# A plan drawn up with other weights: a transformer block with two attentions and a routed feed-forward, ordered by a list planner

## The chip, the cores and the metric

The kernel runs on one core of a Trainium2 chip. The core has a matrix engine (TensorE, PE in the profile, its weight loads PEld), a vector engine (VectorE, DVE), a scalar engine (ScalarE, ACT), GpSimd (POOL) and DMA queues (SyncE, SP, issues most of them). Each engine works through its own list of instructions in order, and semaphores tie the lists together. The metric is the device time of one execution in microseconds; the median of three runs of the kernel before is 718.24 us.

## The reference

Hidden states are 2048 tokens of 128 numbers. With LN a layer norm without weights, the kernel computes:

```
h  = LN(x)
h  = h + global_attention(rmsnorm(h) * w1)      # causal, 16 heads of 8, 4 key heads, latent keys and values
h  = h + local_attention(rmsnorm(h) * w2)       # the same heads, window of 32 tokens
x  = x + LN(h)
f  = LN(x) * gamma + beta
p  = softmax(f @ router.T); e = argmax(p)       # 8 experts
y  = silu(f @ T(sw1)) @ T(sw2) + max(p) * (silu(f @ T(ew1[e])) @ T(ew2[e]))
out = x + LN(y)
```

T() makes weights ternary: round(W / scale) in -1, 0, 1, times the scale of the row. In both attentions queries and keys get a rotary embedding and a norm per head.

## The kernel before

The tokens are worked on in 8 blocks (b = 0 to 7) of 256. For each block there is a front part for each attention (statistics, norm, transposes, projection, a Newton iteration on GpSimd for the head norms, a split into three bf16 parts, an expansion on GpSimd, transposes of keys and queries), the attention itself, an output part, the norms, and the feed-forward. The attention is cut into units (a, b, g, kb): attention a (0 global, 1 local), block b, key head group g of 4, key tile kb. A unit is a score product on TensorE ("qk"), the exponential on ScalarE, for tiles on the diagonal a mask on GpSimd, and later a product with the values ("pv"). Block b has 4 x (2b + 2) global units and 8 local ones, so the work per block grows.

Output steps are "oevac" (ScalarE copies the sums), "oT" (transposes, VectorE divides), "onT" (transposes, ScalarE copies) and "wo" (the output product and residual). Then come "fstat", "fxa", "fh" (the norms) and the 25 steps of ffn_steps: transposes "fhT", router "frouter", "fparts" (bf16 parts on VectorE), "fohT", "fmask" (the one-hot masks are transposed and multiplied into the inputs of the eight experts), first layer "fw1s" and "fw1" with "fz", "fact", "fh1", second layer "fw2" and "fw2s" with "fsel", and "fsum", "fout".

Nothing of the order is written by hand. make_plan() draws up one list of steps, PLAN, when the kernel is built, and each engine then issues its share of every step in that order. The planner keeps books: for each engine the time at which it is free, for three of the PSUM banks and the two score buffers the time at which they come free, and for each step the estimates of COST (engine and us, in order), with HOP = 0.537 us between engines. At every turn it takes the first step of each chain that is allowed (bank count, buffers read), computes the stall that it would cause, 0.98 per us of idle TensorE and 0.432 per us of any other engine, takes off the PULL of its chain, and puts the smallest. The chains are close (output of the global attention), attend (local attention and its output), norms, local (front of the local attention), feed (weight preparation, then feed-forwards), two fronts of the global attention, and the global units themselves as "qk" and "pv". A step of the feed-forward has pull 0, a sum product ("pv") has -0.5.

Filler products are the last part. Before a TensorE step, fillers() works out how long TensorE would be idle by the books. If that is more than KNOBS["idle"], int(idle x share / warm) products of 128x256 bf16 (at most 23) are put ahead of the step as a "warm" entry. They write to the bank or score buffer that the step itself is about to write, so they run after the wait for that bank (L938) and before the wait for the step's inputs:

```
idle = t - free[PE]
return min(KNOBS["most"], int(idle * KNOBS["share"] / KNOBS["warm"])) if idle > KNOBS["idle"] else 0
```

In the plan of before there are 31 such groups with 270 products.

Lines that come up later: L753 the exponential, L837 and L848 transposes and product of a projection, L861 and L870 transposes of keys and queries, L894 score products, L920 products with the values, L938 the fillers, L950 oT, L958 onT, L969 wo, L978 fhT, L987 frouter, L995 fohT, L1005 fmask, L1014 and L1020 fw1s, L1030 fw1, L1041 fw2, L1051 fw2s; on VectorE L1303 fh, L1314 the last of fparts, L1352 fmask, L1393 fsel, L1405 a bank's release in fsum.

Of the kernel before, what the change touches and what calls it, by code (L numbers as in the profile page):

```python
# [96 lines left out]
def weight_steps():  # L97
# [6 lines left out]
PE, DVE, POOL, ACT_E = range(4)  # L104
# [5 lines left out]
    "split": [(DVE, 2.209)], "expand": [(POOL, 2.134)], "kT": [(PE, 0.8), (DVE, 0.6)], "qT": [(PE, 0.55), (DVE, 0.7)],  # L110
    "oT": [(PE, 0.588), (DVE, 0.758)], "onT": [(PE, 0.282), (ACT_E, 0.325)], "wo": [(PE, 0.314), (DVE, 0.411)],
    "oevac": [(ACT_E, 0.3)], "pv": [(PE, 0.388)], "fstat": [(DVE, 1.169), (POOL, 0.662)],
    "fxa": [(DVE, 1.8), (POOL, 2.6)], "fh": [(DVE, 1.275)], "fhT": [(PE, 0.3), (ACT_E, 0.45)],
    "frouter": [(PE, 0.266), (ACT_E, 0.145), (DVE, 1.759)], "fparts": [(DVE, 1.375)],
    "fohT": [(PE, 0.223), (DVE, 1.031)], "fmask": [(PE, 0.647), (DVE, 2.0)], "fw1s": [(PE, 0.539), (DVE, 0.641)],
    "fw1": [(PE, 2.986)], "fz": [(DVE, 0.672)], "fact": [(ACT_E, 1.229)], "fh1": [(DVE, 3.219)], "fw2": [(PE, 6.15)],
    "fsel": [(DVE, 2.303)], "fw2s": [(PE, 0.614)], "fsum": [(DVE, 1.16), (POOL, 1.058)], "fout": [(DVE, 1.296)],
}
HOP = 0.537

STALL_PE, STALL_OTHER = 0.98, 0.432

KNOBS = {
    "idle": 1.372, "share": 0.406, "most": 23, "fronts": 2, "feed": 33.972, "warm": 0.15, "from": 40.0,
}

PULL = {
    "pv": -0.5, "close": 0.896, "local": 0.9, "attend": 0.931, "norms": 1.515, "feed": 0.0, "front": 0.5, "qk": 0.0,
    "evac": 0.3,
}  # L130

# [1333 lines left out]
```

## Time and profile before

| | us |
|---|---|
| median of 3 runs (lowest, highest) | 718.24 (717.93, 720.26) |
| the profiled execution | 721.58 |
| its span, first to last instruction | 719.8 |
| TensorE busy, mean granted clock | 576.0, 0.936 |
| VectorE, ScalarE, GpSimd busy | 405.5, 355.3, 234.2 |

A timeline row has the start, the time taken, the engine, the line, the operation with output and inputs, shapes and count, and in brackets how long the engine had been idle and what ended that.
### The profile page before, as it was taken

The numbers are of one execution on the slowest core, as the hardware profiler recorded it, in microseconds if no ns is written. First come the engines' busy times: TensorE is split into PE (matmuls) and PEld (weight loads), VectorE is DVE, ScalarE is ACT, GpSimd is POOL, SyncE is SP. The second block draws the span as 40 slices with busy tenths as digits, with TensorE's granted clock in tenths as the row PEclk, the third lists the DMA queues.
The fourth block names the chain that finished last, engine by engine and source line by source line (L and its number), as shares of the span: only waits on it lengthen the run. The fifth ranks groups of instructions, "written<-read, shape, count | busy, mean of one in ns | idle before, by whom it ended". The sixth has DMA issues, their size and how long they took to land.

```text
span 719.8 us, 16247 instructions
## 1 busy us (share of the span) xinstructions
PE 576.0 (80%) x6019; PEld 292.9 (41%) x6019; DVE 405.5 (56%) x1054; ACT 355.3 (49%) x490; POOL 234.2 (33%) x624
## 2 busy tenths in 40 slices
PE   2238549968897998989989899888999989947774
PEld 1105235424453442644354353344345433533562
DVE  2654956565475666656665655555536552465275
ACT  1022316854744579448845666565686658301210
POOL 3624782285165237221641112311015120032100
PEclk9999779998999999999999999989999999987897
DMA  8000000000000000000000000000000000000000
GB/s 229 1 1 0 1 2 2 2 1 1 2 2 2 1 10 1 2 1 10 1 2 2 8 3 1 10 1 1 6 5 2 2 9 1 2 0 5 5 0 8
DMA packets 8811, 6.20 MB, mean 9 GB/s; under 512 B 1944, under 2 KB 8096, under 8 KB 8736
## 3 DMA queue, kind: packets, MB, share of 16 engines
q1 hardware_dynamic: 5312, 2.52, 1.3%
q10 hardware_dynamic: 3424, 2.64, 1.3%
q8 instruction: 51, 0.84, 0.5%
q14 instruction: 24, 0.20, 0.1%
HBM read 4.11 MB, written 1.05 MB: 7 GB/s over the span
## 4 chain that ended last, share of the span: by engine, by line
PE 50%; DVE 22%; POOL 13%; issue 8%; ACT 4%; DVEq 0%; SPq 0%; DMA 0%; POOLq 0%; ACTq 0%
PE osum_g L920 14%; PE scores L894 10%; PE misc L1041 5%; PE misc L1030 4%; ACT prob L753 3%; PE scores L888 3%; PE misc L938 3%; PE misc L920 3%; DVE early L1352 2%; PE misc L969 2%; PE misc L870 1%; DVE qT L1246 1%; DVE early L1393 1%; PE misc L861 1%; PE misc L958 1%
## 5 line engine op out<-in xcount | busy, mean ns | idle before, releaser
L753 ACT ACTIVATE prob<-scores 128x1024 f32<-128x1024 f32 (+3 forms) x352 | 307.6, 932 | 191.9 <-PE scores L894 189.0
L920 PE MATMUL osum_g<-prob,V 128*32 128x256 f32 (+1 forms) x2304 | 175.1, 393 | 12.0 <-ACT oTs_g L762 4.8
L894 PE MATMUL scores<-qT,kT 64*128 64x512 bf16 (+3 forms) x760 | 130.1, 363 | 26.1 <-ACT prob L753 12.9
L894 PEld LDWEIGHTS scores<-qT,kT 64*128 64x128 bf16 x760 | 34.9, 94 | 135.7 <-issue 121.7
L693 POOL TENSOR_SCALAR_AFFINE_SELECT prob<-prob 128x512 f32<-128x512 f32 x64 | 41.8, 674 | 142.8 <-ACT prob L753 142.5
L920 PEld LDWEIGHTS osum_g<-prob,V 128*32 128x32 f32 x2304 | 52.9, 111 | 76.2 <-issue 57.3
L938 PE MATMUL misc<-identb 128*128 128x256 bf16 x254 | 40.9, 318 | 24.2 <-DVE kT L1235 9.1
L710 POOL TENSOR_SCALAR frs<-fmv 128x1 f32<-128x1 f32 x16 | 3.4, 210 | 157.3 <-DVE fmv L1409 157.2
L1041 PE MATMUL misc<-t2T,h1p 128*128 128x512 bf16 x192 | 47.3, 398 | 4.4 <-DVE h1p L1386 4.4
L1030 PE MATMUL misc<-early,t1T 128*128 128x256 bf16 x384 | 44.0, 273 | 0.7 <-DVE kT L1235 0.7
L1393 DVE TENSOR_TENSOR early<-misc,oh 128x512 f32<-128x512 f32 x32 | 22.0, 687 | 35.8 <-PE misc L1041 34.6
L938 PEld LDWEIGHTS misc<-identb 128*128 128x128 bf16 x254 | 27.2, 114 | 35.3 <-DVE kT L1235 9.3
L1030 PEld LDWEIGHTS misc<-early,t1T 128*128 128x128 bf16 x384 | 36.8, 98 | 7.2 <-issue 2.8
L1352 DVE TENSOR_TENSOR early<-hp,misc 128x3072 bf16<-128x3072 bf16 x16 | 27.9, 1747 | 19.2 <-PE misc L1005 18.0
L888 PE MATMUL scores<-band,identb 128*128 128x256 bf16 (+2 forms) x128 | 28.5, 304 | 3.9 <-ACT prob L753 3.7
L1041 PEld LDWEIGHTS misc<-t2T,h1p 128*128 128x128 bf16 x192 | 18.5, 102 | 29.0 <-issue 6.5
L1246 DVE COPY qT<-misc 128x1024 bf16<-128x1024 bf16 x32 | 22.1, 691 | 9.2 <-PE misc L870 4.7
L762 ACT COPY oTs_g<-osum_g 128x256 f32<-128x256 f32 x32 | 11.9, 373 | 30.9 <-PE osum_g L920 30.8
L677 POOL TENSOR_SCALAR qe_l<-part_l 128x384 bf16<-128x384 bf16 (+1 forms) x48 | 24.3, 529 | 5.9 <-DVE part_l L1226 5.9
L677 POOL TENSOR_SCALAR qe_g<-part_g 128x384 bf16<-128x384 bf16 (+1 forms) x48 | 22.4, 488 | 4.8 <-DVE part_g L1226 4.8
L920 PE MATMUL misc<-prob,V 128*32 128x160 f32 (+1 forms) x736 | 23.8, 262 | 0.0
L642 POOL TENSOR_TENSOR rs_l<-mv_l 128x2 f32<-128x2 f32 x8 | 1.5, 193 | 65.3 <-DVE mv_l L1164 65.3
(214 smaller groups left out, 807.1 us busy)
## 6 DMA issues: line engine op xcount, KB each, us to landing
X<-in_L_attn_hidden_dram SPq DMA_DIRECT2D x8, 128.0 KB, 4.6
early<-in_L_ffn_expert_w_dram ACTq DMA_DIRECT2D x1, 1024.0 KB, 7.3
out_dram<-X SPq DMA_DIRECT2D x16, 64.0 KB, 1.5
rope<-in_rope_dram SPq DMA_DIRECT2D x1, 256.0 KB, 3.6
early<-in_L_ffn_shared_w_dram ACTq DMA_DIRECT2D x2, 128.0 KB, 8.2
wraw_l<-in_L_attn_l_wq_dram ACTq DMA_DIRECT2D x1, 64.0 KB, 2.6
ident<-in_ident_dram SPq DMA_DIRECT2D x1, 64.0 KB, 2.5
wraw_g<-in_L_attn_g_wq_dram SPq DMA_DIRECT2D x1, 64.0 KB
```

The costliest lines, as they stand in the source:

```text
L677: pool.tensor_scalar(qe[a][:, i, :, lo:lo + n, :], src.unsqueeze(2).broadcast_to([P, H, n, HD]), 1.0, 0.0, ALU.mult, ALU.add)
L693: pool.affine_select(out=d, in_=d, compare_op=ALU.is_ge, fill=0.0, base=0, pattern=[[0, 4], [1, P]], channel_multiplier=-1).then_inc(mask_ ...
L753: act.activation(prob[:, n % NP, :, lo:hi], src, ACT.Exp, scale=float(HD) ** -0.5).then_inc(exp_done, 1)
L888: pe.matmul(o[:, :, lo:end], identb[:], bias.unsqueeze(1).broadcast_to([P, 2, end - lo]), start=True, stop=False, skip_group_check=True)
L894: ins = pe.matmul(o[:, :, c:c + w], kT[a][rows, g, P * (t % kept[a]):P * (t % kept[a]) + P], qT[a][rows, b % Q_KEPT[a], 2 * g:2 * g + 2, q ...
L920: ins = pe.matmul(o[32 * m:32 * m + 32, q:q + w], V[a][:, t % kept[a], g, :], prob[:, n % NP, j, c:c + w], start=(first and k == 0), stop= ...
L938: pe.matmul(room, identb[:], identb[:].unsqueeze(1).broadcast_to([P, 2, P]), start=True, stop=True)
L1030: ins = pe.matmul(bank(s)[:, 0:QB], t1T[:, FT * e + f, :], hm[:, e, p, :], start=(e == 0 and p == 0), stop=(e == NE - 1 and p == 2))
L1041: ins = pe.matmul(bank(s, j)[:], h1p[:, p, FT + f, P * i:P * i + P], t2T[:, f, 4 * j:4 * j + 4, :].rearrange("p e d -> p (e d)"), start=(p ...
L1246: dve.tensor_copy(qT[a][:, b % Q_KEPT[a], :, P * i:P * i + P], bank(s)[:].bitcast(BF16).rearrange("p (m q) -> p m q", m=H // 2)).then_inc( ...
L1352: link(dve.tensor_tensor(hm[:, :, :, P * i:P * i + P], h.unsqueeze(1).broadcast_to([P, NE, 3, P]), m.unsqueeze(2).broadcast_to([P, NE, 3, ...
L1393: link(dve.tensor_tensor(sel[:, 4 * j:4 * j + 4, :], bank(s, j)[:].rearrange("p (e d) -> p e d", e=4), oh[:, i, 0, 4 * j:4 * j + 4].unsque ...
```

## The change

It alters numbers in the planner's tables and nothing else. In COST: fh on VectorE 1.275 to 1.58; fhT; fw1s; fw1 2.986 to 3.404; fz; fw2 6.15 to 5.916; fsel; fsum; fout 1.296 to 0.884. In KNOBS: the threshold of a filler group 1.372 to 1.889, share over warm from 0.406/0.15 to 0.394/0.129, the earliest time of the feed chain 33.972 to 30.371, the time from which fillers are allowed 40.0 to 32.165. In PULL: close 0.896 to 0.66, norms 1.515 to 1.43.

```diff
-    "fxa": [(DVE, 1.8), (POOL, 2.6)], "fh": [(DVE, 1.275)], "fhT": [(PE, 0.3), (ACT_E, 0.45)],
+    "fxa": [(DVE, 1.8), (POOL, 2.6)], "fh": [(DVE, 1.58)], "fhT": [(PE, 0.257), (ACT_E, 0.675)],
     "frouter": [(PE, 0.266), (ACT_E, 0.145), (DVE, 1.759)], "fparts": [(DVE, 1.375)],
-    "fohT": [(PE, 0.223), (DVE, 1.031)], "fmask": [(PE, 0.647), (DVE, 2.0)], "fw1s": [(PE, 0.539), (DVE, 0.641)],
-    "fw1": [(PE, 2.986)], "fz": [(DVE, 0.672)], "fact": [(ACT_E, 1.229)], "fh1": [(DVE, 3.219)], "fw2": [(PE, 6.15)],
-    "fsel": [(DVE, 2.303)], "fw2s": [(PE, 0.614)], "fsum": [(DVE, 1.16), (POOL, 1.058)], "fout": [(DVE, 1.296)],
+    "fohT": [(PE, 0.223), (DVE, 1.031)], "fmask": [(PE, 0.647), (DVE, 2.0)], "fw1s": [(PE, 0.624), (DVE, 0.998)],
+    "fw1": [(PE, 3.404)], "fz": [(DVE, 0.614)], "fact": [(ACT_E, 1.229)], "fh1": [(DVE, 3.219)], "fw2": [(PE, 5.916)],
+    "fsel": [(DVE, 2.299)], "fw2s": [(PE, 0.614)], "fsum": [(DVE, 1.218), (POOL, 1.433)], "fout": [(DVE, 0.884)],
 }
 HOP = 0.537
 
 STALL_PE, STALL_OTHER = 0.98, 0.432
 
 KNOBS = {
-    "idle": 1.372, "share": 0.406, "most": 23, "fronts": 2, "feed": 33.972, "warm": 0.15, "from": 40.0,
+    "idle": 1.889, "share": 0.394, "most": 23, "fronts": 2, "feed": 30.371, "warm": 0.129, "from": 32.165,
 }
 
 PULL = {
-    "pv": -0.5, "close": 0.896, "local": 0.9, "attend": 0.931, "norms": 1.515, "feed": 0.0, "front": 0.5, "qk": 0.0,
+    "pv": -0.5, "close": 0.66, "local": 0.9, "attend": 0.931, "norms": 1.43, "feed": 0.0, "front": 0.5, "qk": 0.0,
     "evac": 0.3,
 }
```

## Rows read from the trace of the kernel before

**Rows 1.** The page: span, busy time of the engines, granted clock in 40 slices.

```profile
span 719.8 us, 16247 instructions
...
PE 576.0 (80%) x6019; PEld 292.9 (41%) x6019; DVE 405.5 (56%) x1054; ACT 355.3 (49%) x490; POOL 234.2 (33%) x624
...
PEclk9999779998999999999999999989999999987897
```

**Rows 2.** Busy time by stage: start, middle, end.

```profile
core 0: us, PE busy (x) PEld busy (x) DVE busy (x) ACT busy (x) POOL busy (x), PEclk, DMA share, GB/s
0.00:125.00 125.00, 64.56 (x605) 37.22 (x605) 72.10 (x205) 30.25 (x49) 63.70 (x177) 0.92 0.12 34
125.00:618.00 493.00, 442.31 (x4849) 210.47 (x4847) 276.09 (x713) 312.46 (x417) 155.91 (x405) 0.96 0.01 3
618.00:719.80 101.80, 69.17 (x575) 45.18 (x567) 57.28 (x138) 12.59 (x24) 14.58 (x43) 0.85 0.01 4
```

**Rows 3.** The same view of four of the 14 stretches with a low clock.

```profile
74.00:79.00 5.00, 4.36 (x22) 2.93 (x23) 4.58 (x19) 1.60 (x3) 4.02 (x14) 0.66 0.00 0
...
412.00:417.00 5.00, 4.30 (x30) 2.90 (x30) 2.56 (x11) 1.88 (x3) 1.42 (x3) 0.66 0.01 3
...
641.00:652.00 11.00, 5.91 (x23) 3.40 (x24) 6.43 (x15) 0.00 (x0) 7.22 (x21) 0.53 0.00 1
...
702.00:707.00 5.00, 4.57 (x17) 1.86 (x18) 1.15 (x3) 0.00 (x0) 0.00 (x0) 0.66 0.01 3
```

**Rows 4.** Timeline of the start: filler products and one vector instruction.

```profile
start us, us, engine line op out<-in xcount [idle before <-releaser]
58.81 3.86 PE L938 MATMUL misc<-identb 128*128 128x256 bf16 x23
...
62.50 0.35 DVE L1175 TENSOR_SCALAR Hn<-X,mv_g,rs_g 128x128 f32<-128x128 f32 x1 [14.90 <-POOL rs_g L638]
...
103.09 5.09 PE L938 MATMUL misc<-identb 128*128 128x256 bf16 x23 [9.10 <-DVE kT L1235]
```

**Rows 5.** Timeline of TensorE: filler groups, each with the product behind it.

```profile
362.14 0.61 PE L938 MATMUL misc<-identb 128*128 128x256 bf16 x4 [0.98 <-DVEq L1354]
362.68 0.64 PE L861 MATMUL misc<-identb,ke_g 128*64 128x128 bf16 x16
...
583.40 0.98 PE L938 MATMUL misc<-identb 128*128 128x256 bf16 x4 [2.52 <-DVEq L1405]
584.16 0.64 PE L958 MATMUL misc<-ident,on_l 128*128 128x128 f32 x2
...
620.83 0.72 PE L938 MATMUL misc<-identb 128*128 128x256 bf16 x5 [0.94 <-DVEq L1354]
621.48 0.39 PE L1014 MATMUL misc<-ohT,s1pT 24*128 24x256 bf16 x2
...
646.09 3.81 PE L938 MATMUL misc<-identb 128*128 128x256 bf16 x17 [7.14 <-DVEq L1395]
```

**Rows 6.** Timeline of TensorE: output of the global attention, block 5.

```profile
412.70 0.61 PE L958 MATMUL misc<-ident,on_g 128*128 128x128 f32 x2 [1.85 <-DVEq L1263]
```

**Rows 7.** Groups by line: busy us, mean ns of one, idle before.

```profile
L1041 PE MATMUL misc<-t2T,h1p 128*128 128x512 bf16 x192 | 47.3, 398 | 4.4 <-DVE h1p L1386 4.4
...
L1303 DVE TENSOR_SCALAR fh<-X,fmv,frs 128x128 f32<-128x128 f32 x16 | 5.1, 354 | 6.2 <-POOL frs L706 3.3 <-PE misc L978 2.2 <-DVE on_g L1260 0.3
```

**Rows 8.** Timeline of the feed-forward of block 6, from its rows to its masks.

```profile
592.69 0.60 DVE L1303 TENSOR_SCALAR fh<-X,fmv,frs 128x128 f32<-128x128 f32 x2 [1.10 <-POOL frs L706]
...
597.60 0.44 PE L978 MATMUL misc<-ident,fh 128*128 128x128 f32 x2
...
603.74 0.42 DVE L1314 TENSOR_TENSOR hp<-hres,hp 128x256 bf16<-128x256 f32 x1
...
616.23 1.07 PE L1005 MATMUL misc<-identb,oh 128*128 128x128 bf16 x16
...
616.97 1.75 DVE L1352 TENSOR_TENSOR early<-hp,misc 128x3072 bf16<-128x3072 bf16 x1 [9.84 <-PE misc L1005]
```

## The prediction, made before the changed kernel was run

> **What bounds the kernel now.** I read the page's busy line first, then busy time by stage, then the stretches with a low granted clock, then the timeline around the filler products and in the drain. TensorE is busy for 576.0 of 719.8 us and no other engine passes 56% [rows 1]. By stage it is not one kernel [rows 2]. Up to 125 us TensorE is busy 64.6 of 125 us: the start waits for chains of small steps. From 125 to 618 us it is busy 442.3 of 493 us: here the attention products set the pace and only 50.7 us of idle time can be won. 
>
> **The change, part by part.** No instruction of the computation is added or removed, and no wait is edited. What changes is the order in which the four engines' lists are filled, and the number of filler products. I followed the planner's rules through the order of before with the old weights, and asked at each choice how far the new ones push it. I did not draw up the new plan.
>
> *Start, up to 125 us: nothing but fillers.* The feed chain's earliest time falls from 33.97 to 30.37, but before that the other candidates still win (its lead over them is negative until the same step), so weight preparation stays at its place in VectorE's list. The books of VectorE are 3.6 us earlier after it, which moves all candidates near it alike. The first product group is then planned into a gap of 5.6 instead of 9.2, so 17 fillers for 23. In the trace those 23 take from 58.81 to 62.5 us, but VectorE waits for GpSimd until 62.50 anyway [rows 4]: worth 0. The next group grows from 12 to 14. The group of 23 at 103.09 us runs at the low clock, 5.09 us, straight after a bank wait of 9.10 us [rows 4]; its planned gap is far over the cap of 23 in both, so it stays. Sum of the start: +0.2 us, with -5.1 (that group gone) as the low end and +5.1 (one more such group) as the high one.
>
> *Fillers, rest.* The rule was int(gap x 0.406/0.15) for gaps over 1.372, and is int(gap x 0.394/0.129) for gaps over 1.889, capped at 23: 3.05 instead of 2.71 products per planned us. Of the 31 groups (270 products) of before, 13 have planned gaps below 1.889 (all groups of 3 and 4, and one of 5): 47 products go. Of the other 18, 13 grow, by 19 in sum. A group costs only where it runs after the last thing its step waited for. Three of the dropped ones visibly do: 4 at 362.14 us after a bank wait, next product 0.54 us later; 4 at 583.40, next product 0.76 later; 5 at 620.83, next 0.65 later [rows 5]. That gives -1.95 us; if none of it reached the end it is 0, and if all 47 counted at the 0.13 us each of the first of those rows it is -6.1. The grown ones cost per product 0.107 us (11 in the 5.09/23 = 0.22 at the low clock): of the 19, some 13 stand directly ahead of their step, four of them at the low clock behind long waits as at 646.09 [rows 5]: 9 x 0.107 + 4 x 0.22 = +1.8 us (0 to 4.2, all 19 at 0.22).
>
> *Less pull for global outputs (0.896 to 0.66).* Each such step may now cost 0.236 less planned stall before attention work is taken ahead of it. Of the 32 choices for it in the plan of before six were won by less than 0.236. Only one of those six stands behind a long real wait: the transposes of the global output of block 5 at 412.70 us, 1.85 us idle [rows 6], and the low clock of 412 to 417 us follows it, 1.7 us lost [rows 3]. Its planned margin over the next score product was 0.06, so it flips; with a score product first the wait is filled. -3.55 us; 0 at worst if the next bank wait takes its place, and a delay of local work behind it could eat it.
>
> *Longer feed-forward estimates.* Per block the planner now books 1.2 us more for the chain of 25 steps and 0.41 us more of TensorE. This is no better fit: the normalised rows take 2 x 0.354 = 0.71 us on VectorE where the books go from 1.275 to 1.58, and the wide products of the second layer take 47.3/16 = 2.96 us a step [rows 7] where 5.916 stands for 6.15. The effect is that feed-forward steps are put a little later in the lists. In the middle that is cheap or useful, since TensorE has attention work to put first: I take one mask wait of the kind at 362.14 (0.98 us idle before it [rows 5]) as gone, -1.0 us. The bounds are -7 (a seventh of the 50.7 us of idle time [rows 2], about what one more step of slack at each of seven blocks can reach at that wait's size) and +3 (three such waits new).
>
> *Clock.* Without the short groups, the gaps that they stood in become idle. One more low stretch at the price of the one at 412 us: +1.7 us; from 0 to three, +5.1. The Trainium skill, "TensorE: Matmul & The Clock Gate", section "HAM oscillation — how this bites in real kernels", describes just this: waits between bursts of products take the clock down, and the return is paid each time. By that rule keeping short fillers would be worth more than their run time, which speaks against this change. The trace agrees only in part, since the groups at 362.14 and 620.83 us ran at full clock behind waits under 1 us [rows 5], and the sum does not rest on it.
>
> *Drain.* The phase of block 6 decides here. Its normalised rows are ready at 593.29 us, the transposes of them come at 597.60, the last operand of the masks is ready at 604.16, but the mask transposes come at 616.23, with VectorE idle for 9.84 us before it uses them [rows 8]. The planner held them: a sum product costs 0.5 in its choice and the mask step 0.511 as long as VectorE is idle, which is 0.432 x (0.647 + 0.537), terms that the change leaves alone. So that hold stays unless block 6 moves against the borders between head groups. I take 0 here and leave both directions to the rivals.
>
> Sum: +0.2 - 1.95 + 1.8 - 3.55 - 1.0 + 1.7 = -2.8, rounded by the drift of all the small moves to -3.0 us: 718.6 us profiled, and on the median 718.24 - 3.0 = 715.2 us.
>
> **Rivals.**
> A (forecast): the orders stay alike, small gains win: 715.2 us, its own range 711 to 719.
> B (slower): block 6 comes late. Head groups of block 7 follow one another and the router steps are let in only at their border. If the longer books (fh +0.305, fhT +0.225) or the delayed global output of block 6 make it miss the border before the last group, then the router chain, 597.60 to 604.16 = 6.6 us [rows 8], is run in the drain, where little covers it: 718.2 + 6.6 - 1 = 724 us. For it: everything in the change moves this chain later, and the margin of the global output of block 6 was 0.20. Against: its rows lay ready for 4.3 us before they were used, so it has slack. It decides where the mask operands are complete later than about 616 us.
> C (slower): the clock. Three more low stretches: 715.2 + 5.1 - 1.7 = 718.6 and, if a third of such a wait as the 9.10 us at 103 us comes on top, 722. Against: fillers cover few of the present waits.
> D (faster): block 6 comes a head group earlier, so the masks and the first layer run under the attention. Then the wait of 7.14 us at 646.09 [rows 5] and most of the low clock of 641 to 652 us (11 x 0.47 = 5.2 lost, [rows 3]), with nearly no work under it, shrink: 7.14 + 1.8 us of filler and product at the low clock = 9: 708 us. The same would follow if only VectorE's selection step came ahead of the local split at 643 us. For it: more planned time per block shifts the phase by 0.41 x 6 = 2.5 us, against a head group's length of some 12. Against: most shifts are later ones.
> E (no effect): the plan differs but the gains are taken back at the next wait: 718.2 us.
>
> **How the numbers follow.** A 0.45, B 0.19, C 0.11, D 0.17, E 0.08. Faster by over 0.3% (under 716.1): A 0.34, D 0.17, C 0.01 = 0.52. Within: A 0.10, C 0.03, E 0.05 = 0.18. Slower (over 720.4): A 0.01, B 0.19, C 0.07, E 0.03 = 0.30. The range must reach D and B, since each holds more than is to be left out with the other: 705 to 725 us. It includes the unknown of the start (5.1 either way) only in part.
>
> **What would show it.** Right: some 242 fillers or a few less for 270, none in groups of 3; start to 125 us within 0.5 us; no wait before the global output of block 5; masks of block 6 still behind the last sums of block 7; 13 to 16 low stretches. Wrong: another order already in the first 125 us, a last local attention that starts more than 5 us later or earlier, or a third of the fillers in new places.

## The result, and the profile after

The changed kernel takes 711.55 us (median of 4 runs, 710.75 to 712.70) beside 718.38 us for the kernel before on the same chip: a ratio of 0.9901, 95% interval 0.9877 to 0.9925. The profiled run took 710.75 us, its span is 708.1 us. The forecast was 715.2 us, faster, with 705 to 725 us as its range. The sign holds and the time lies in the range, but the change is -6.8 us where -3.0 was forecast, and the sum behind the forecast does not hold, as the experiments show.

The page of the changed kernel, in the lines that answer to [rows 1]:

```profile
span 708.1 us, 16154 instructions
...
PE 561.2 (79%) x5966; PEld 287.2 (41%) x5981; DVE 404.8 (57%) x1054; ACT 354.2 (50%) x490; POOL 233.8 (33%) x624
...
PEclk9999669997999999999999999999999999979797
```

Busy time by stage in the changed kernel, then three short stretches (columns as in [rows 2], which the first three rows answer; the fourth answers the 412 us row of [rows 3]):

```profile
core 0: us, PE busy (x) PEld busy (x) DVE busy (x) ACT busy (x) POOL busy (x), PEclk, DMA share, GB/s
0.00:125.00 125.00, 65.87 (x599) 36.82 (x599) 72.56 (x206) 30.40 (x50) 64.31 (x178) 0.90 0.12 34
125.00:603.00 478.00, 427.04 (x4805) 204.51 (x4815) 271.28 (x699) 311.68 (x417) 154.11 (x404) 0.98 0.01 3
603.00:708.10 105.10, 68.32 (x565) 45.83 (x567) 60.99 (x150) 12.15 (x24) 15.41 (x43) 0.84 0.01 3
412.00:417.00 5.00, 4.81 (x62) 2.62 (x62) 3.40 (x6) 3.88 (x6) 1.02 (x2) 1.00 0.01 3
626.00:637.00 11.00, 5.82 (x47) 4.77 (x48) 6.02 (x10) 0.63 (x1) 5.12 (x11) 0.53 0.00 0
```

VectorE, ScalarE and GpSimd have the same busy time as before to 1.1 us. TensorE has 14.8 us less, and the granted clock of the middle is 0.98 instead of 0.96. The middle is 15 us shorter and the last stage 3.3 us longer, but these stages don't hold the same steps in both kernels.

**A ruler that holds the same steps.** I used three moments of TensorE's list that all orders share: the product of block 5's global output (L969, 413.99 us before, 413.56 after), the same product of block 6 (528.69 and 519.12), and the last turn of a global sum, block 7's (L950, 618.79 and 601.57). Up to the products of blocks 5 and 6 the two lists have put the same set of steps, but for three. First the kernel before, then the changed one, between these moments and to the end:

```profile
413.99:528.69 114.70, 103.74 (x1052) 49.85 (x1050) 59.12 (x138) 70.94 (x91) 21.86 (x53) 0.93 0.01 4
528.69:618.79 90.10, 84.44 (x937) 37.02 (x933) 42.25 (x109) 64.18 (x82) 17.92 (x45) 0.96 0.01 3
618.79:719.80 101.01, 68.44 (x564) 44.97 (x564) 56.56 (x137) 12.22 (x23) 14.58 (x43) 0.85 0.01 4
```

```profile
413.56:519.12 105.56, 97.50 (x1045) 45.81 (x1046) 59.43 (x138) 69.87 (x90) 20.36 (x51) 0.98 0.02 4
519.12:601.57 82.45, 77.40 (x892) 33.76 (x893) 36.87 (x94) 62.72 (x80) 17.14 (x45) 1.00 0.01 3
601.57:708.10 106.53, 69.75 (x576) 47.17 (x579) 61.54 (x152) 12.15 (x24) 15.41 (x43) 0.84 0.01 3
```

Read these as follows. Up to block 5's output nothing is won (0.4 us). Between the outputs of blocks 5 and 6 the work is the same, and 9.1 us go: TensorE is busy 6.2 us less for the same products, since the clock is 0.98 instead of 0.93, and idle 2.9 us less (10.96 to 8.06). In block 7's global attention 7.65 us go, but 15 vector instructions go with them (109 to 94 there, 137 to 152 behind it). By the two lists these belong to five steps of block 6's feed-forward: the router, its bf16 parts, the turn of the one-hot masks and the two masks. They stood ahead of block 7's last global turn and now stand behind it, in the drain, which is 5.5 us longer. These two together are worth 2.1 us (191.11 to 188.98). By this ruler the profiled gain of 11.7 us is 0.4 + 9.1 + 2.1. The profiled run of before was itself 3.3 us over its median, so of the 11.7 some 7 are the kernel's (6.8 by the medians).

### The profile page after: what moved, and what is told of

It is laid out like the page before. It is cut to its first block, busy times and chain, and to the rows that moved or that the text cites. A ratio compares the mean times of both kernels' runs of the same rounds, so it can differ in the third digit from the quotient of the medians.

```text
span 708.1 us, 16154 instructions
## 1 busy us (share of the span) xinstructions
PE 561.2 (79%) x5966; PEld 287.2 (41%) x5981; DVE 404.8 (57%) x1054; ACT 354.2 (50%) x490; POOL 233.8 (33%) x624
## 4 chain that ended last, share of the span: by engine, by line
PE 43%; DVE 22%; POOL 17%; issue 10%; ACT 6%; DVEq 1%; SPq 0%; DMA 0%; POOLq 0%; ACTq 0%
PE osum_g L920 11%; PE scores L894 8%; PE misc L1041 5%; ACT prob L753 5%; PE misc L1030 4%; PE scores L888 3%; PE misc L920 3%; POOL qe_l L677 2%; PE misc L938 2%; DVE early L1352 2%; DVE qT L1246 2%; POOL ke_l L682 2%; PE misc L870 1%; PE misc L969 1%; DVE early L1393 1%
## 5 line engine op out<-in xcount | busy, mean ns | idle before, releaser
L753 ACT ACTIVATE prob<-scores 128x1024 f32<-128x1024 f32 (+3 forms) x352 | 307.5, 931 | 177.4 <-PE scores L894 174.7
L920 PE MATMUL osum_g<-prob,V 128*32 128x256 f32 (+1 forms) x2304 | 172.9, 390 | 12.0 <-ACT oTs_g L762 4.4
L894 PE MATMUL scores<-qT,kT 64*128 64x512 bf16 (+3 forms) x760 | 127.0, 355 | 26.2 <-ACT prob L753 12.7
L1041 PE MATMUL misc<-t2T,h1p 128*128 128x512 bf16 x177 | 44.1, 400 | 7.9 <-DVE h1p L1386 3.1
L1030 PE MATMUL misc<-early,t1T 128*128 128x256 bf16 x384 | 45.0, 275 | 0.3 <-DVE kT L1235 0.3
L938 PE MATMUL misc<-identb 128*128 128x256 bf16 x221 | 34.3, 320 | 11.1 <-DVE kT L1235 7.1
L1030 PEld LDWEIGHTS misc<-early,t1T 128*128 128x128 bf16 x384 | 37.2, 99 | 7.3 <-issue 2.6
L1352 DVE TENSOR_TENSOR early<-hp,misc 128x3072 bf16<-128x3072 bf16 x16 | 28.0, 1753 | 15.2 <-PE misc L1005 13.5
L938 PEld LDWEIGHTS misc<-identb 128*128 128x128 bf16 x221 | 24.1, 114 | 19.7 <-DVE kT L1235 7.3
```

Source lines behind the costliest of these rows:

```text
L753: act.activation(prob[:, n % NP, :, lo:hi], src, ACT.Exp, scale=float(HD) ** -0.5).then_inc(exp_done, 1)
L894: ins = pe.matmul(o[:, :, c:c + w], kT[a][rows, g, P * (t % kept[a]):P * (t % kept[a]) + P], qT[a][rows, b % Q_KEPT[a], 2 * g:2 * g + 2, q ...
L920: ins = pe.matmul(o[32 * m:32 * m + 32, q:q + w], V[a][:, t % kept[a], g, :], prob[:, n % NP, j, c:c + w], start=(first and k == 0), stop= ...
L938: pe.matmul(room, identb[:], identb[:].unsqueeze(1).broadcast_to([P, 2, P]), start=True, stop=True)
L1030: ins = pe.matmul(bank(s)[:, 0:QB], t1T[:, FT * e + f, :], hm[:, e, p, :], start=(e == 0 and p == 0), stop=(e == NE - 1 and p == 2))
L1041: ins = pe.matmul(bank(s, j)[:], h1p[:, p, FT + f, P * i:P * i + P], t2T[:, f, 4 * j:4 * j + 4, :].rearrange("p e d -> p (e d)"), start=(p ...
```

## The experiments

Each kernel was run beside the kernel before on the same chip. The pooled medians of the kernel before were 718.37, 717.42, 717.91 and 720.57 us for the four groups in which they stand here: the two splices and the two filler kernels; the two single edits and the first two edits of the drain; one weight alone and the third edit of the drain; no fillers. The segments named are those of the ruler. No kernel leaves out part of the computation; the filler products are no part of it.

**1. Which part of the list: two splices.** One list up to the 999th step (fillers not counted), then the other. The edit (`plan_by` draws up the list with one kernel's weights, `cut` parts it at that step), here for the first; the second has the names exchanged:

```diff
-PLAN = make_plan()
+PLAN = cut(plan_by("before"))[0] + cut(plan_by("after"))[1]
```

> The plan of the kernel before for its first 999 steps (fillers not counted), that of the changed kernel for the rest. At this point both have put the same set of steps, and score product 610 of 760 runs there: at 534.3 us before, at 522.9 us in the changed kernel, after which both take 185 us. Theory O (the gain of 6.8 us comes from the order of the middle): about 718, product 610 at 534 us. Theory D (it comes from the other interleaving of local attention 6 and the last global attention): about 711 to 713. Theory F (it comes from the filler set alone): in between, 715 to 718.

> The plan of the changed kernel for its first 999 steps, that of the kernel before for the rest. Theory O: product 610 near 523 us and about 707 to 712 in all, the end taking its 185 us. Theory D: 718. Theory F: in between.

Measured: old head with new tail 716.24 us (714.88 to 721.08), ratio 0.9973 (0.9948 to 0.9999); new head with old tail 717.13 us (713.97 to 719.46), ratio 0.9972 (0.9947 to 0.9997). Each half brings some 0.3% alone, 0.5% at the most by its interval; the whole brings 1%. In time both land in the 715 to 718 us that theory F had given for the first, but the next experiment rules F out. Theory O's 707 to 712 us for the second falls, though score product 610 comes where O had it: at 532.8 us and at 524.6 us (534.3 before, 522.9 changed). The trace of each still tells the halves apart. Between the outputs of blocks 5 and 6, old head, then new head:

```profile
413.95:527.18 113.23, 101.99 (x1046) 48.44 (x1051) 59.10 (x139) 70.96 (x91) 21.93 (x53) 0.94 0.01 4
```

```profile
413.78:520.82 107.04, 98.96 (x1045) 46.70 (x1046) 59.62 (x138) 69.99 (x90) 20.43 (x51) 0.97 0.02 4
```

The new head has its gain up to block 6's output. It loses 3.4 us of it in block 7's attention, where the new head with the old tail takes 93.54 us (90.10 before, 82.45 changed). Part of that is the seam, a wait of 2.13 us for a normalised tile that neither whole kernel has, with a granted clock of 0.57 over the 8 us from 527 us on (L895 is L837 here):

```profile
527.98 0.69 PE L895 MATMUL misc<-ident,xn_l 128*128 128x128 f32 x2 [2.13 <-DVE xn_l L1238]
```

So the second splice is no clean measure of its tail. The first shows the new tail behind the old head: 83.6 us to the last global turn and 107.2 us behind it, 190.8 together, beside 191.1 before and 189.0 changed.

**2. Which fillers: the order of one kernel with the filler rule of the other.**

```diff
-    "idle": 1.372, "share": 0.406, "most": 23, ... "warm": 0.15, "from": 40.0,
+    "idle": 1.889, "share": 0.394, "most": 23, ... "warm": 0.129, "from": 32.165,
```

The second kernel has the changed order and the old rule. `feed` stays with the order in each.

> The order of the kernel before, with the new filler rule alone: 18 groups and 242 products instead of 31 and 270. The prediction's filler and clock terms (-1.95, +1.8, +1.7) give +1.5: 720. Theory F gives 711 to 714, with the low-clock stretches of 412, 457 and 474 us gone. Theory O gives 717 to 719.

> The order of the changed kernel, with the old filler rule (31 groups, 263 products). Theory F: 716 to 718. Theory O: 710 to 713, and product 610 near 523 us.

Measured: the old order with 242 fillers by the new rule 723.35 us (721.7 to 724.05), ratio 1.0059 (1.0039 to 1.0079); the new order with 263 by the old rule 711.69 us (710.18 to 711.95), ratio 0.989 (0.9862 to 0.9918). The change of rule costs 5 us on the old order, which lies above all three expectations, and on the new one nothing that can be told (by the ratios 0.8 us, with intervals that overlap). It is no part of the gain, so theory F falls. Where the 5 us lie is open: the profiled run of the old order with the new rule has a span 2.5 us over that of before, and 1.8 us of them are in the drain. The new rule came with one more number, the earliest time of the feed chain, which no run changes alone. A list drawn up with it alone differs from that of before in nine places, all among steps 38 to 46 of 1261, so it can't have made the new order of the middle. Between the outputs of blocks 5 and 6, old order and new order:

```profile
413.73:528.85 115.12, 103.56 (x1051) 50.25 (x1053) 59.10 (x138) 70.87 (x91) 21.94 (x53) 0.93 0.01 4
```

```profile
415.53:520.74 105.21, 97.37 (x1044) 46.34 (x1045) 59.41 (x138) 69.84 (x90) 20.42 (x51) 0.98 0.02 4
```

Three profiles of the old order give 114.7, 113.2 and 115.1 us for this segment. The seven of the new order in this study (changed kernel, new head, old fillers, three kernels with an edited drain, no fillers) give 104.2 to 107.0. The order makes this segment, with any of the filler sets that were run.

**3. The one flip that the forecast had priced.** The kernel before with block 5's turn behind two score products. This is how the list stands before and after; the edit itself moves these steps:

```diff
-("onT", 0, 5), ("qk", 0, 6, 0, 12), ("qk", 0, 6, 0, 13), ("wo", 0, 5)
+("qk", 0, 6, 0, 12), ("qk", 0, 6, 0, 13), ("onT", 0, 5), ("wo", 0, 5)
```

> The order before with one edit: the turn of block 5's global output (412.70 us in the trace before, TensorE waits 1.85 us for VectorE there, and 5 us of low clock follow) is put behind the two score products that came right behind it, as the changed plan has it; the fillers are those before. The forecast's reason (this one flip is worth 3.55 us, since the products fill the wait and the low clock goes with it): 714.8 us, score product 500 of 760 at about 449 us instead of 452.4, and no low clock between 410 and 420 us. Rival, the middle is faster for many small reasons of which this is one: the wait shrinks from 1.85 to about 1.4 us and the clock dips at another place instead, 717 to 718.5 us, product 610 at 532 to 534 us. Third: the low clock at 412 us is not due to this wait, and the time stays within 0.3% with product 450 at 413 us.

Measured: 716.77 us (714.6 to 721.37), ratio 0.9996 (0.9976 to 1.0016): no change. TensorE's timeline at the flip, and the stretch around it in the same kernel (L967 is L958 of the kernel before):

```profile
410.24 0.50 PE L903 MATMUL scores<-qT,kT 64*128 64x512 bf16 x4
412.16 0.44 PE L967 MATMUL misc<-ident,on_g 128*128 128x128 f32 x2 [1.42 <-DVEq L1272]
...
411.00:417.00 6.00, 4.38 (x34) 2.88 (x34) 3.84 (x12) 2.19 (x4) 2.37 (x6) 0.72 0.00 0
```

The changed kernel at the same place:

```profile
410.27 0.50 PE L894 MATMUL scores<-qT,kT 64*128 64x512 bf16 x4
412.19 0.44 PE L958 MATMUL misc<-ident,on_g 128*128 128x128 f32 x2 [1.42 <-DVEq L1263]
...
411.00:417.00 6.00, 4.81 (x62) 2.62 (x62) 4.02 (x9) 4.88 (x7) 1.22 (x2) 1.00 0.01 3
```

The forecast's 714.8 us falls. Of the rival expectation the wait holds: the two score products are 0.50 us of work and leave 1.42 of the 1.85 us of wait [rows 6]. But the low clock comes at the same place and not at another one, and the time is within 0.3%, as the third expectation had it. Up to that turn the two traces are alike; behind it one has a clock of 0.72 over 6 us and the other 1.00.

It could be that the work behind the wait decides, since the changed kernel has more of it in that stretch (its next two score products and one mask turn stand ahead of the output's product: 4.81 us, 62 matmuls, for 4.38 us, 34). The kernel of experiment 5 with the estimates alone speaks against it. Its list is that of before from 13 steps ahead of this turn to 61 steps behind it, the flip is not made, the wait is as long as before, and the clock stays at 1.00:

```profile
412.00 0.44 PE L958 MATMUL misc<-ident,on_g 128*128 128x128 f32 x2 [1.86 <-DVEq L1263]
...
411.00:417.00 6.00, 4.38 (x50) 2.37 (x50) 3.96 (x11) 3.98 (x6) 2.50 (x6) 1.00 0.00 0
```

So the low clock at 412 us follows neither from the length of this wait nor from the steps next to it. What decides it is open, and a price for it can't be hung on this flip.

**4. The largest wait of that segment.** The old list with only the 21 steps around block 4's first expert products (`fw1`) in the new order:

```diff
-..., ("oevac", 0, 6, 2), ("fw1", 4, 0), ("fz", 4, 0), ("fh1", 4, 0), ("fw1", 4, 1), ("fz", 4, 1), ("fact", 4, 1), ...
+..., ("fw1", 4, 0), ("fz", 4, 0), ("fh1", 4, 0), ("pv", 0, 6, 2, 6), ("fw1", 4, 1), ("fz", 4, 1), ("qk", 0, 6, 2, 10),
+..., ("fact", 4, 1), ("fh1", 4, 1), ..., ("oevac", 0, 6, 2)
```

What is wrong there is seen in the kernel before, TensorE first and ScalarE below:

```profile
492.12 5.41 PE L1030 MATMUL misc<-early,t1T 128*128 128x256 bf16 x48
497.47 0.50 PE L894 MATMUL scores<-qT,kT 64*128 64x512 bf16 x4
500.71 1.53 PE L938 MATMUL scores<-identb 128*128 128x256 bf16 x10 [2.75 <-ACT prob L753]
...
499.12 0.63 ACT L788 ACTIVATE early<-early 128x512 f32<-128x512 f32 x1 [6.50 <-DVEq L1375]
499.65 1.49 ACT L753 ACTIVATE prob<-scores 128x1024 f32<-128x1024 f32 x2
```

ScalarE's list has the tanh of the second half (L788) ahead of the exponential of the next score product. The two halves run back to back for 5.41 us, ScalarE stands idle for 6.50 us before that tanh, the scores computed at 497.47 us can't be exponentiated before it, and TensorE waits 2.75 us.

> The order before with only the 21 steps around the first expert products of block 4 taken from the changed plan: the two halves of them (5.41 us back to back at 492.12 us before) stand apart with sums and scores between them, and ScalarE's tanh of the second half stands ahead of an exponential that does not wait for it. Theory that ScalarE's list is what stops TensorE there (it waits 2.75 us at 500.71 us for an exponential behind a tanh that waits for the second half, and low clock follows): the wait falls to about 1 us, score product 560 of 760 comes 2.5 to 4 us earlier than 497.5 us, the time is 714.5 to 716 us. Rival, the wait is paid at another place, since ScalarE or VectorE is as late for the next products: product 560 within 1 us of 497.5 and 717.5 to 719 us.

Measured: 719.0 us (712.42 to 720.02), ratio 1.0005 (0.9968 to 1.0042). The place itself does as expected: the wait is 1.01 us (in this kernel L1044 is L1030, L952 is L938, L767 is L753), as in the changed kernel, score product 560 comes 2.6 us earlier, and the segment takes 110.36 us for 114.70 at a clock of 0.97.

```profile
485.79 2.79 PE L1044 MATMUL misc<-early,t1T 128*128 128x256 bf16 x24
...
489.08 2.79 PE L1044 MATMUL misc<-early,t1T 128*128 128x256 bf16 x24
...
496.40 1.38 PE L952 MATMUL scores<-identb 128*128 128x256 bf16 x11 [1.01 <-ACT prob L767]
...
413.06:523.42 110.36, 99.55 (x1046) 48.19 (x1050) 59.13 (x139) 70.86 (x91) 21.66 (x53) 0.97 0.01 4
```

The total does not follow: two of the six runs lie at 712.4 and 714.2 us, four at 718.2 to 720.0. Where the local gain goes in the four, the profile doesn't say beyond its own run, in which the drain took 103.09 us for 101.01. In time the rival's upper edge of 719 us holds. That the order of these steps makes this wait is shown; that undoing it makes the kernel faster is not.

**5. One weight alone.** The kernel before with the changed estimates (`COST`) only, and with the changed pull (`PULL`) only.

```diff
-    "fh": [(DVE, 1.275)], "fhT": [(PE, 0.3), (ACT_E, 0.45)], ...
+    "fh": [(DVE, 1.58)], "fhT": [(PE, 0.257), (ACT_E, 0.675)], ...
```

```diff
-    "close": 0.896, ... "norms": 1.515,
+    "close": 0.66, ... "norms": 1.43,
```

> The kernel before with the changed step estimates alone; pull and filler rule stay. Its list has the drain of the changed kernel step by step (masks of block 6 ahead of the local projection, both expert halves around the local turns), while around block 5's global output and block 4's first expert products it stands as before: the turn ahead of the two score products, the two halves back to back. It has 279 fillers in 33 places. Theory that the gain lies in those places of the middle and comes with the pull: score product 610 of 760 at 531 to 535 us (534.3 before, 522.9 changed), a low clock again at 412 us, 715 to 719 us. Rival, the forecast's term for longer estimates (1.0 us at most) is far too small and they bring most of it: product 610 under 528 us and 709 to 713 us.

> The kernel before with the changed pull for global outputs and norms alone; estimates and filler rule stay. Its list has both flips of the middle (block 5's turn behind the two score products, the expert halves of block 4 apart), a drain of its own (masks of block 6 ahead of the second half by 19 steps as before, the first half two steps ahead of the turned keys) and 278 fillers in 30 places. Theory that the pull makes the middle faster: product 610 at 523 to 527 us, and with the drain of before 709 to 713 us. Rival, the two weights bring it only together, since each alone leaves waits of the other kind: product 610 at 528 to 532 us and 714 to 717 us.

Measured: estimates alone 715.69 us (712.18 to 721.53), ratio 0.9978 (0.9945 to 1.001); pull alone 721.14 us (715.7 to 724.82), ratio 1.0055 (1.0021 to 1.0088). The estimates alone land at the lower edge of the time of their first expectation, but not by its reason: the low clock at 412 us did not come again (experiment 3), and product 610 of 760 comes at 528.2 us, which neither expectation had. The pull alone is slower than either of its expectations; of these the rival, that the weights bring it only together, holds in kind, though product 610 comes at 523.7 us as the first one had it. The segments, estimates alone and then pull alone:

```profile
412.90:524.38 111.48, 101.55 (x1056) 47.63 (x1060) 59.11 (x139) 71.95 (x92) 21.86 (x53) 0.95 0.02 4
524.38:606.83 82.45, 78.34 (x900) 34.30 (x900) 36.84 (x94) 62.74 (x80) 17.15 (x45) 1.00 0.01 3
606.83:710.40 103.57, 68.86 (x587) 48.31 (x589) 61.52 (x152) 12.15 (x24) 15.41 (x43) 0.87 0.01 3
```

```profile
412.80:519.81 107.01, 96.84 (x1057) 46.21 (x1058) 59.42 (x138) 70.84 (x91) 20.70 (x51) 1.00 0.02 4
519.81:607.46 87.65, 80.95 (x915) 36.57 (x914) 42.24 (x109) 62.00 (x80) 17.97 (x45) 0.98 0.01 3
607.46:714.00 106.54, 68.05 (x574) 45.99 (x576) 56.48 (x137) 12.23 (x23) 14.22 (x43) 0.84 0.01 3
```

The pull makes most of the gain in the segment before block 6's output (107.0 us for 114.7), though the estimates alone bring 3.2 us there too (111.5). The estimates take block 6's five steps out of block 7's attention (82.45 us and 94 vector instructions, exactly as in the changed kernel). With the pull alone these steps stay there (109 instructions) and the drain is 5.5 us longer all the same, with TensorE waiting 13.56 us for the turned local keys at 651.86 us. That is why the pull alone loses what it wins: 191.1 us behind block 6's output before, 194.2 with the pull, 186.0 with the estimates, 189.0 with both. One thing is left over: both profiled runs were the fastest of their kernels (712.18 and 715.70 us), so the slower runs, 3.5 and 5.4 us longer at the median, hold a loss that no trace here shows.

**6. The drain of the changed kernel.** VectorE's list has block 6's masks (L1352, 611.39 to 615.13 us) ahead of block 7's local projection, and behind that projection TensorE waits 9.09 us for the turned keys at 631.18 us. The idea is that the end hangs on the chain that the projection starts. The first edit puts the masks behind it; the second kernel also puts the second expert half of block 6 ahead of block 7's local turns, and block 7's local output ahead of the first `fsum` of block 6, and so ahead of the second-layer products of its second half, whose banks are not yet free; the third also puts block 7's norms and the turn of its feed-forward input ahead of block 6's last selection, its router ahead of block 6's last output, and drops 23 fillers. `moved` takes steps out of the list and puts them ahead of the one named last.

```diff
+PLAN = moved(PLAN, [("fmask", 6, 0), ("fmask", 6, 1)], ("split", 1, 7))
```

```diff
+PLAN = moved(PLAN, [("warm", 8, "fw1", 6, 1), ("fw1", 6, 1), ("fz", 6, 1), ("fact", 6, 1)], ("kT", 1, 7))
+PLAN = moved(PLAN, [("onT", 1, 7), ("wo", 1, 7), ("fstat", 7)], ("fsum", 6, 0))
```

```diff
+PLAN = moved(PLAN, [("fxa", 7), ("fh", 7), ("fhT", 7)], ("fsel", 6, 1))
+PLAN = moved(PLAN, [("frouter", 7), ("fparts", 7)], ("fout", 6, 1))
+PLAN.remove(("warm", 23, "fhT", 7))
```

> The changed kernel with one edit behind the middle: the two masks of block 6 (3.74 us on VectorE from 611.39 us) are put behind the projection of block 7's local attention, so that they run while GpSimd does its three Newton steps (VectorE idle for 4.67 us there). Theory that the drain is one chain, local projection, Newton, turns, local attention, feed-forward of block 7: the turned keys come 3 to 3.5 us earlier than 631.18 us and the time is 708 to 708.5 us. Rival, the masks now delay the first expert products of block 6 and these the drain: 710.5 to 712.5 us. A second rival: a longer stretch at the low clock takes the gain back, 710 to 711.5 us.

> The changed kernel with three edits in the drain: the masks behind the local projection as in the kernel with that edit alone, the second half of block 6's first expert products with its evacuation and tanh ahead of block 7's local turns (TensorE waits 9.09 us for them, the half costs 3.46 us behind them), and the turn and product of block 7's local output ahead of block 6's second expert sum, whose banks are not free (TensorE waits 2.84 us at 654.48 us, and the output's turn at 658.32 us stands behind it though its input is ready at 653.04 us). Theory of the one chain: 3.3 us for the masks, 3 to 5 for the half, 3 to 4 for the output, so 700 to 703 us. Rival, the drain has two chains and block 6's feed-forward holds block 7's (VectorE's shared tiles, the banks): not under 706 us. With the low clock over more of the drain, where TensorE now has longer waits in one piece: 704 to 707 us.

> The changed kernel with the three edits of the drain before (706.55 us) and two more: block 7's norms and the turn of its feed-forward input stand ahead of block 6's last selection on VectorE (3.3 us of it lie between the output and the norms there), the router of block 7 ahead of block 6's last output, and the 23 fillers before that turn are gone, since block 6's expert sum now covers them. Theory that what is left in the drain is VectorE's list, not a dependence: the turn of the feed-forward input comes 4 to 6 us earlier and the time is 701 to 703 us. Rival, the selection only moves behind the turn and holds the router by as much, 704.5 to 707 us. Second rival, without those fillers the clock is low over the last block: 705 to 709 us.

Measured: 707.37 us (704.38 to 708.03), ratio 0.9872 (0.9853 to 0.9891); 706.55 us (704.6 to 707.15), ratio 0.9853 (0.9832 to 0.9874); 702.71 us (701.61 to 703.68), ratio 0.9796 (0.9772 to 0.982). TensorE's turned keys in the changed kernel and with the first edit (L869 there), then the drain with the third kernel:

```profile
631.18 1.06 PE L861 MATMUL misc<-identb,ke_l 128*64 128x128 bf16 x16 [9.09 <-POOL ke_l L682]
```

```profile
627.04 0.64 PE L869 MATMUL misc<-identb,ke_l 128*64 128x128 bf16 x16 [0.36 <-POOL ke_l L690]
```

```profile
604.57:701.90 97.33, 68.03 (x553) 44.55 (x556) 60.48 (x152) 12.46 (x24) 13.74 (x43) 0.84 0.01 4
```

With the masks behind, the keys come 4.1 us earlier and the ratio goes from 0.9901 to 0.9872 (2.1 us; the medians, from different chips, differ by 4.2). The two intervals overlap a little, the runs themselves do not (704.38 to 708.03 beside 710.75 to 712.70). So the masks were on the chain to the end. The next two edits bring 0.8 us more on the same chip, which is within the noise, and far from the 700 to 703 us expected of the one chain; the rivals' 704 to 707 us hold. The output's product comes at 649.46 us for 659.16, and block 7's normalised rows at 662.34 for 667.11, with block 6's last selection ahead of them on VectorE. With that list mended and 23 fillers dropped, the turn of the feed-forward input comes 2.6 us earlier still (660.38 us for 663.00), and the last kernel is at 702.71 us, 2.0% faster than the kernel before and by the ratios 1.1% faster than the changed one (0.9796/0.9901): the best kernel of the study. Its expectation of 701 to 703 us holds.

**7. No fillers at all.** The changed order with `"most": 0`.

> The changed kernel without any of its 232 filler products; the order of all other steps is untouched. Theory that fillers matter through the clock in the start and the drain: 46 of them stand ahead of the first long gaps, some 150 in the drain, and without them the low clock covers more of both, 715 to 725 us. Rival, that the fillers are nearly worth nothing on this order (263 and 232 of them gave the same time): 710 to 714 us. The middle has one group of them, so score product 610 stays 420 to 425 us behind product 50 of 760 either way (404.6 us in the changed kernel's profile, some 2 us more if the start's clock shifts into it).

Measured: 707.84 us (706.12 to 714.74), ratio 0.9868 (0.9799 to 0.9937), beside 0.9901 for the changed kernel: the intervals overlap, so the fillers bring nothing that can be told here. The first expectation, 715 to 725 us, falls; the rival was too high by some 2 us. From score product 50 to product 610 the kernel takes 404.0 us, for 404.6 in the changed one; the 420 to 425 us in the expectation contradict the 404.6 beside them and were wrong. The old order was not run without fillers. From its profile, the page's clock and the last segment:

```profile
PEclk9965568997998999999999999999999999669666
...
599.55:704.60 105.05, 57.34 (x436) 35.89 (x436) 61.57 (x152) 12.15 (x24) 15.48 (x43) 0.72 0.01 3
```

In the drain the clock falls from 0.84 to 0.72, 140 filler products are gone, TensorE is busy 12.4 us less, and the segment is 1.5 us shorter. So in the drain the fillers do hold the clock up, and cost about as much time as they save.

## Why the prediction was right, and where its sum was wrong

**Start (+0.2 us): right.** Groups of 17, 14 and again 23, and the vector instruction that waits for GpSimd till 62.57 us [rows 4]. The global output of block 0 comes at 68.15 us (67.86 before), that of block 1 at 140.50 (140.26). The order there is not quite that of before: nine places of the list are exchanged by the earlier time of the feed chain (experiment 2). The forecast had named another order in the first 125 us as a sign against it; it did no harm.

**Dropped and grown fillers (-1.95 and +1.8) and their clock (+1.7): mis-sized, and conditional.** Together they were +1.6 us. On the old order the new rule costs 5.0 us, on the new order -0.1 by the medians and 0.8 by the ratios. The count is 232 in 17 groups, not 242 in 18, since the drain's list is another one. But 14 of the 17 groups stand ahead of steps that had one before; three, with 46 products, are new, all in the drain. That is less than the third which the forecast had named as a sign against it.

**Pull (-3.55): the flip came, the price did not.** The step that failed is "with a score product first the wait is filled": the wait is 1.42 us, and the low clock behind it stays when this flip is made alone (experiment 3: 0.9996). What the runs show in its place is a whole segment that gets shorter, block 6's attention, with the clock up in it: -9.1 us in the changed kernel, -7.7 us with the pull alone, -1.6 and -4.3 us with the two single places tried. I had bounded this term by one wait and one low stretch, and taken it for granted that this wait caused that stretch; with the estimates alone the wait is there and the low stretch is not.

**Clock (+1.7): wrong in sign.** By a count in windows of 1 us of all stretches under 1.00 with work in them, the kernel before has 17 (I had counted 14) and 42.7 us lost, the changed one 11 and 34.1 us. Between 125 us and the last global sum it is 10 stretches and 20.5 us against 3 and 8.5. The reason given, that idle gaps left by short fillers would take the clock down, is answered by experiment 7: without any filler the middle is as fast as ever (segments of 104.15 and 82.48 us). The rule of the Trainium skill ("TensorE: Matmul & The Clock Gate", section "HAM oscillation — how this bites in real kernels"), by which waits between bursts are paid for each time, bore on it from the other side. The trace agrees in part: between the outputs of blocks 5 and 6 TensorE is idle 8.06 us for 10.96, and the clock is 0.98 for 0.93; but waits of equal length are followed by a low clock in one kernel and not in another.

**Longer estimates (-1.0): size in bounds, mechanism not seen.** I expected a mask wait less in the middle. Instead they move the five steps of block 6, its router to its masks, into the drain (82.45 for 90.10 us, then 106.53 for 101.01), and alone they are worth 2.2 us, with an interval that includes none.

**Drain (0): wrong, and rival B's mechanism came in.** The turn of block 6's masks comes at 610.67 us for 616.23 [rows 8], which looks early. But everything there is 17 us earlier, and against block 7's last global turn the masks are late: 2.6 us ahead of it before, 9.1 us behind it now. Block 6's rows are turned at 600.07 us, its router runs at 602.50 us, behind that global turn at 601.57 us, and the mask operands are complete at 606.97 us. This is what B described: the router chain misses the attention and runs in the drain. Its price of 6.6 us is near the 5.5 us by which the drain is longer. Its sign, operands later than 616 us, was a time of the kernel before and could not tell. Its total of 724 us fails because 16.8 us went at the same time between the output of block 5 and the last global turn (7.65 of them with the five steps gone from there). D, with the masks under the attention, is the opposite of what happened, and its 708 us is not what its own numbers give (718.2 - 9 = 709.2).

Of its signs of being right the forecast had the start and the groups of 3 gone; the wait before block 5's output is still there (1.42 us), and the low stretches are 11, not 13 to 16. Of its signs of being wrong, besides the order at the start, block 7's local projection starts 18.7 us earlier (611.56 us for 630.26).

So the sign came out right, and the time inside a range 20 us wide, through several errors that offset one another: a pull term of -3.55 where the segment gave -9.1 in the profiled pair, nothing for the drain, and a clock term with the wrong sign. That is in part luck. The last 0.2 of the -3.0 us, "the drift of all the small moves", is in no row. Part of the 9.1 may be the profiled run's own excess over the median, though the old order with the new fillers, profiled 0.7 us above its median, shows the same segment at 115.1 us. What stays open: which steps besides the two tried make the rest of block 6's segment, what decides whether a wait is followed by a low clock, and why single edits that are seen to work in a trace leave the median where it was.

## What to carry to other kernels

When a planner's weights change, price the segment between two steps that both orders share, not the choices one by one: single flips worth 1.6 and 4.3 us in their own segment were worth nothing in the total, and two weights worth -2.2 and +3.2 us alone gave -6.8 together (with the new filler rule, which is worth nothing on that order). Look on each engine for a step that waits for something late while standing ahead of one whose operands are ready: ScalarE's tanh ahead of an exponential, VectorE's masks ahead of a projection; moving such steps by hand in the drain, and dropping 23 fillers, gave as much again (0.9901 to 0.9796) as all the new weights (1 to 0.9901). Before tuning a rule for filler products, leave them all out once: here 232 of them bring nothing that can be told. And give a sign that decides between rivals as a place in the order, not as a time: a step can come earlier by the clock and later against the work that was to cover it.

## What the runs showed of the hardware that I had not expected

**The mean granted clock is no measure of time.** Without fillers it is 0.903 and the span is 704.6 us; with them 0.947 and 708.1 us. Part of that is the record itself. From 39 to 57.4 us the two kernels run the same list at the same times; first the changed kernel, then the one without fillers:

```profile
39.00:57.40 18.40, 8.21 (x64) 2.29 (x64) 8.00 (x27) 6.97 (x11) 5.80 (x10) 1.00 0.00 1
```

```profile
39.00:57.40 18.40, 8.22 (x64) 2.30 (x64) 8.00 (x27) 6.97 (x11) 5.81 (x10) 0.50 0.00 1
```

The busy times agree within 0.01 us and the recorded clock is 1.00 in one and 0.50 in the other. A group of four score products takes 0.82 us in both at 46.8 us, where at 410 us it takes 0.50. So TensorE ran at the low level in both, and in the changed kernel the record doesn't show it. The clock of the first 60 us should be read from durations, and means over a whole run should not be compared to a hundredth.

**Equal waits, unequal clocks.** A wait of 2.03 us for the same local turn is followed by a mean clock of 0.66 in the kernel before and by 1.00 in the changed one, with the same steps around it (12 of the list up to it, 19 behind it). First the kernel before, then the changed one:

```profile
314.08 0.66 PE L958 MATMUL misc<-ident,on_l 128*128 128x128 f32 x2 [2.03 <-DVEq L1405]
...
313.00:318.00 5.00, 3.92 (x15) 1.98 (x16) 2.35 (x10) 2.80 (x5) 1.93 (x4) 0.66 0.00 2
```

```profile
314.06 0.41 PE L958 MATMUL misc<-ident,on_l 128*128 128x128 f32 x2 [2.03 <-DVEq L1405]
...
313.00:318.00 5.00, 3.88 (x21) 1.93 (x22) 2.57 (x10) 2.74 (x4) 2.40 (x6) 1.00 0.01 2
```

At 412 us it is the same: behind 1.42 us the clock is 0.72 in one kernel and 1.00 in another, and behind 1.85 and 1.86 us it is 0.72 and 1.00 with the same steps before and after (experiment 3). So the price of a wait in clock can't be read off its length.
